# Moving the combining of the first experts' results into the experts' own block of a graph and mixture-of-experts kernel

## The chip, the cores and the metric

The kernel runs on one core of one Trainium2 chip. The metric is the device time of one execution in microseconds (us), from start to end on that core. Lower is better. TensorE is called PE, VectorE DVE, ScalarE ACT, GpSimd POOL and SyncE SP; SPq, ACTq and POOLq are their instruction queues, from which they also issue transfers.

## What is computed

The input x is 3125 rows of 256 numbers. Four layers follow one another, each added to its input, which is normalised (LayerNorm without a gain) beforehand: a graph network of three steps, a first mixture of experts (16 experts, 512 wide, the best two taken for each row), a second graph network with relations, and a second mixture (8 experts, 1024 wide). The change is about the end of the first mixture and the start of the second graph layer:

```python
def _L0_ffn_ref(x, gate_w, gate_b, w1, b1, w2, b2, gamma, beta):
    ...
    topk_w = jax.nn.softmax(topk_vals, axis=-1)
    h = jax.nn.relu(jnp.einsum('bsh,ehf->bsef', x, w1) + b1)
    expert_out = jnp.einsum('bsef,efh->bseh', h, w2) + b2
    sel = jnp.take_along_axis(expert_out, topk_idx[:, :, :, None], axis=2)
    moe = jnp.sum(topk_w[..., None] * sel, axis=2)
    y = x + moe
    mu = jnp.mean(y, axis=-1, keepdims=True)
    var = jnp.var(y, axis=-1, keepdims=True)
    return (y - mu) / jnp.sqrt(var + EPS) * gamma + beta
...
x = x + _L0_ffn_ref(_layernorm(x, axis=-1)[None], ...)[0]
x = x + _L1_gnn_ref(_layernorm(x, axis=-1), edge_index, edge_type_500, ...)
```

The second graph layer gathers a row of h = LayerNorm(x), scaled by a factor of the source node's degree, for each of 103,125 edges, multiplies it by a relation's row and sums by destination. It also needs h itself, for the part of the update that does not pass through the edges.

## The kernel before

Rows are held as NT = 25 tiles of 128 rows, in NJ = 5 groups of J = 5 tiles. `c.x` (in the profile `parts_and_x`) is the running sum, `c.xn` (`xn`) the normalised rows that the experts took in, `c.h` (`h`) the normalised rows for the second graph layer.

**Experts (`experts`, `feed_forward`, L1893).** The rows are sorted by expert into 64 tiles. POOL gathers tile t+4 (L2301) while PE computes tile t: a transpose (L2025), the first product (L2037), the second (L2056); ACT applies the activation (L2122); DVE adds the expert's bias and leaves the result in one of four buffers `f_yb` (L2243); POOL scatters the buffer to DRAM `ys` (L2290), each row to the place of its token, once for the token's first choice and once for its second. POOL at last waits until the scatters have landed, and the block ends. A block ends with all five engines meeting. Then, where a `Core` closes, POOL clears the semaphores that it owned, one after the other, while the others wait (L125), and all meet again.

**Combining (`combine_and_norm`, L2362), a block of its own.** SP reads `ys` back into `got`, ten transfers (five groups, two choices, L2393), then waits for a memset of POOL (L2385), reads the two short tails (L2397), then gamma (L2398) and beta (L2399), both spread over 128 partitions. DVE clips the degrees, ACT takes their root (L2438), and DVE inverts them. DVE waits for gamma and beta, adds beta to all of x (L2514), and goes through the groups in this order, which is written out by hand:

```python
for i in range(NJ):
    sum_up(i)
    if i:
        join(i - 1)
    scale_first(i)
    if i:
        scale_next(i - 1)
join(NJ - 1)
scale_next(NJ - 1)
```

`sum_up` forms y = xn + w0*got0 + w1*got1 (L2472) and its moments (L2456 to L2464); `scale_first` inverts the root that ACT took of the variance (L2412, L2481, L2482); ACT normalises y in place (L2422). `join` multiplies by gamma (L2487), adds to x (L2488) and takes the moments of the new x; `scale_next` makes the next scales (L2497 to L2504). ACT then writes five tiles of rows for the table that the second layer gathers from (L2431, `out`) and, behind them, five tiles of `c.h` (L2435). SP stores each group's `out` (L2403) and waits for the stores; the block and its `Core` end.

**Second graph layer (`aggregate`, L618, and `Beside`, L2565).** 416 steps n of two gathers each (POOL, L705). ACT makes the places of step n (L665, L668) up to six steps ahead of PE, DVE multiplies by the relation's row (L775), PE sums by destination (L794), DVE adds up (L757). Beside these, every 14 steps from step 48 on, one tile of `c.h` goes through a product: PE transposes it (L2612) at step n, ACT copies the transpose (L2633) at step n+4, PE multiplies at n+5 (L2618), DVE adds it to x at n+9 (L2645).

The second experts (L1893 again, with `out` given) end otherwise than the first: there SP itself waits for the scatters (L2284) and then issues the copies of the result (L2016).

Of the kernel before, what the change touches and what calls it, by code (L numbers as in the profile page):

```python
# [7 lines left out]
ALU = mybir.AluOpType  # L8
# [1873 lines left out]
def experts(nc, c, I, name, ne, nf, tiles, softmax_first, w1, b1, w2, b2, logits, xn_table, norm, act_fn, combine_rows, relation=None, out=None):  # L1882

    ys = c.dram(f"{name}_ys", [NP + P if out is not None else 2 * NP + tiles * P, D])
    with Core(nc) as k:
        weight = k.sb(f"{name}_weight", [P, 2, NT])
        slot = k.sb(f"{name}_slot", [P, 2, NT], I32)
        feed_forward(nc, c, name, ne, nf, tiles, softmax_first, logits, w1, b1, w2, b2, norm, act_fn, relation, weight, slot, xn_table, ys, out)
        if combine_rows:
            combine_rows(ys, weight, c.xn)  # L1890


def feed_forward(nc, c, name, ne, nf, tiles, softmax_first, logits, w1, b1, w2, b2, norm, act_fn, relation, weight, slot, xn_table, ys, out):  # L1893
# [9 lines left out]
    with Core(nc) as k:  # L1903
# [17 lines left out]
        low_hit = k.sb(f"{name}_low_hit", [P, 2, NT, P], BF16)  # L1921
        tile_hit = k.sb(f"{name}_tile_hit", [P, 2, NT, tiles], BF16)
        named = k.sb(f"{name}_named", [P, 2, NT, 2, tiles], BF16)
        token_f, token = k.sb(f"{name}_token_f", [P, tiles]), k.sb(f"{name}_token", [P, tiles], I32)
        work = RelationRows(nc, c, k, f"{name}_rr", *relation, True) if relation else None
# [27 lines left out]
        if norm:  # L1953
# [9 lines left out]
            k.sem(f"{name}_e{x}") for x in ("xt", "xT", "h", "hT", "y", "yb", "asked", "ask"))  # L1963
        with nc.Block() as block:  # L1964
# [12 lines left out]
            def _(sp):  # L1977
# [114 lines left out]
            def _(act):  # L2092
# [6 lines left out]
                if not softmax_first:  # L2099
                    act.wait_ge(s_a, 1)  # L2100
                    nc.scalar.activation(small[:, 1, :], small[:, 0, :], ACT.Exp).then_inc(s_b, 1)
                act.wait_ge(s_etab, 1)
                act.wait_ge(s_bias, 16 * len(loads))
                with act.Fori(0, tiles // 2) as i:
                    for s in range(2):
# [12 lines left out]
                        for f in range(FC):  # L2118
                            if f % BF == 0:
# [3 lines left out]
                                                 bias=b1s[:, bass.ds(e, 1), f]).then_inc(s_hT, 1)  # L2123

            @block.vector
            def _(dve):
# [99 lines left out]
                else:  # L2226
# [5 lines left out]
                    v.tensor_tensor(weight[:, 1, :], weight[:, 0, :], small[:, 1, :], ALU.mult)  # L2232
                dve.wait_ge(s_bias, 16 * len(loads))
                dve.wait_ge(s_etab, 1)
                if out is None:
                    dve.sem_inc(s_yb, 2)
                    for t in range(tiles):
                        e = dve.value_load(e_tab[0:1, 0, t:t + 1], min_val=0, max_val=ne - 1)
                        dve.wait_ge(s_y, t + 3)
                        if t >= Y:  # L2240
# [3 lines left out]
                            .then_inc(s_yb, 1)  # L2244
                else:
# [26 lines left out]
            def _(pool):  # L2272
                asked = 0
                if work:
                    while asked < BEFORE:
                        work.both(pool, asked)
                        asked += 1
# [15 lines left out]
                if out is not None:  # L2293
                    pool.wait_ge(s_home, 1)
                    pool.wait_ge(s_start, 32)
                for t in range(tiles):
# [12 lines left out]
                    if work and t >= Q - 1:  # L2309
                        upto = BEFORE + (work.pairs - BEFORE) * (t - Q + 2) // (tiles - Q + 1)  # L2310
                        while asked < upto:
                            work.both(pool, asked)
                            asked += 1
# [8 lines left out]
                if work:  # L2322
                    work.store(pool, work.pairs - 2, work.pairs)
                    work.stored(pool)
# [37 lines left out]
def combine_and_norm(nc, c, name, I, ys, weight, xn, h_table):  # L2362
# [3 lines left out]
    with Core(nc) as k:  # L2366
        k.got = k.sb(f"{name}_got", [P, 2, NT, D])
        k.s_got = [k.sem(f"{name}_got{i}") for i in range(NJ)]
# [389 lines left out]
```

## Time and profile before

| | |
|---|---|
| median of three runs | 3142.7 us (3141.61, 3142.7, 3150.35) |
| the profiled execution, its own time | 3142.47 us |
| its span in the trace | 3140.8 us |
| busy, share of the span | PE 78%, DVE 57%, POOL 56%, ACT 46% |
| mean granted TensorE clock | 0.91 of full speed |
| first experts, 64 tiles | about 1063 to 1377 us |
| combining | 1379.5 us to the stage below |
| second graph layer, first instruction | 1490.17 us |

Times in the trace count from the span's start. The span leaves out 1.7 us of the execution's own time. The execution that was profiled lies 0.2 us under the median.

### The profile page before, as it was taken

The page shows a single profiled execution, that of the slowest core. Times are in us where ns is not written, and L with a number is a line of the kernel's source. Part 1 is how long each engine was busy: PE and PEld are TensorE (multiplying, and loading weights), DVE is VectorE, ACT ScalarE, POOL GpSimd, SP SyncE. Part 2 cuts the span into 40 slices and gives each one's busy share as a digit, 9 for nine tenths or more (in the row PEclk, how much of TensorE's full clock was granted, in tenths as well). Part 3 has the DMA queues.
Part 4 walks back from the last instruction along what each step waited for, and adds up shares of the span by engine and source line. Part 5 has one row for each costly group of instructions (what it writes and reads, how often), then busy time and mean ns, then how long its engine had stood idle before and what let it go on. Part 6 is the DMA issues. An engine that isn't in the chain of part 4 may idle for free. (4 is left out here: it accounts for less than half of the span.)

```text
span 3140.8 us, 53019 instructions
## 1 busy us (share of the span) xinstructions
PE 2446.1 (78%) x14195; PEld 1912.7 (61%) x14195; DVE 1785.5 (57%) x5112; ACT 1454.7 (46%) x3766; POOL 1747.2 (56%) x1701
## 2 busy tenths in 40 slices
PE   1549999989998489840587787778777767699997
PEld 1226666667777488740465565555555545699996
DVE  5649989847788511018676666666666666401110
ACT  0247767645665333315544444444434434355553
POOL 1547777667774045420777777777777760133332
PEclk9979999999999599975899999998999897799998
DMA  5657777568885233431766666666666642243232
GB/s 204 232 161 218 231 222 213 171 215 258 262 251 170 81 120 108 160 115 44 221 189 186 186 189 178 186 184 186 184 180 184 181 135 99 90 130 75 51 63 65
DMA packets 289373, 516.56 MB, mean 164 GB/s; under 512 B 79344, under 2 KB 137057, under 8 KB 287084
## 3 DMA queue, kind: packets, MB, share of 16 engines
q0 software_dynamic: 86192, 225.20, 28.0%
q1 hardware_dynamic: 184380, 265.72, 25.8%
q10 hardware_dynamic: 18544, 22.59, 2.2%
q8 instruction: 116, 1.90, 0.2%
q14 instruction: 141, 1.16, 0.1%
HBM read 381.08 MB, written 137.11 MB: 165 GB/s over the span
## 5 line engine op out<-in xcount | busy, mean ns | idle before, releaser
L705 POOL DMA_INDIRECT agg_r_rows<-h_table,parts_and_x x832 | 832.2, 1000 | 364.9 <-issue 227.4
L794 PE MATMUL agg_r_sums<-agg_r_rows,agg_r_onehot 128*128 128x257 f32 x1664 | 497.8, 428 | 255.7 <-DVE agg_r_rows L775 162.9
L794 PEld LDWEIGHTS agg_r_sums<-agg_r_rows,agg_r_onehot 128*128 128x128 f32 x1664 | 312.6, 207 | 395.0 <-issue 315.8
L665 ACT ACTIVATE agg_r_gap<-iota,parts_and_x 128x128 f32<-128x128 f32 x832 | 286.8, 392 | 450.2 <-PE agg_r_sums L794 421.2
L757 DVE TENSOR_TENSOR acc<-acc,agg_r_sums 128x257 f32 (+1 forms) x834 | 351.5, 421 | 134.5 <-PE agg_r_sums L794 47.4
L1651 POOL DMA_INDIRECT rl_buf<-r_table,kinds x288 | 315.4, 1095 | 140.4 <-issue 72.0
L2037 PEld LDWEIGHTS f_pH<-f_xT,f_w 128*128 128x128 f32 x2816 | 329.7, 193 | 36.4 <-ACT f_xT L2116 15.6
L2037 PE MATMUL f_pH<-f_xT,f_w 128*128 128x128 f32 x2816 | 343.5, 279 | 7.5 <-ACT f_xT L2113 4.6
L808 PE MATMUL agg_r_spread<-xn 128*128 128x257 bf16 x2664 | 344.5, 289 | 0.0
L2056 PE MATMUL f_pY<-f_w,f_hT 128*128 128x256 f32 x1408 | 324.3, 380 | 9.0 <-DMA f_w<-in_L_ffn_w 9.0
L808 PEld LDWEIGHTS agg_r_spread<-xn 128*128 128x128 bf16 x2664 | 276.4, 104 | 72.2 <-issue 8.8
L2122 ACT ACTIVATE f_hT<-f_pH,f_b 128x128 f32<-128x128 f32 x704 | 198.1, 373 | 260.9 <-PE f_pH L2037 260.6
L1456 PE MATMUL la_acc<-la_parts,la_counts 128*128 128x512 f32 x1250 | 309.1, 404 | 12.0 <-DVE la_parts L1563 12.0
L1651 POOL DMA_INDIRECT rm_buf<-r_table,kinds x250 | 245.9, 984 | 88.2 <-issue 69.2
L2056 PEld LDWEIGHTS f_pY<-f_w,f_hT 128*128 128x128 f32 x1408 | 258.3, 190 | 41.1 <-DMA f_w<-in_L_ffn_w 10.8
L1456 PEld LDWEIGHTS la_acc<-la_parts,la_counts 128*128 128x128 f32 x1250 | 235.0, 190 | 72.7 <-issue 25.0
L2301 POOL DMA_INDIRECT f_xb<-xn_table,f_token x120 | 118.5, 988 | 267.7 <-DVE f_token L2206 116.5
L1370 DVE TENSOR_SCALAR b_oh<-b_numbers,b_code 128x400 bf16<-128x400 f16 x980 | 253.5, 323 | 0.0
L775 DVE TENSOR_TENSOR agg_r_rows<-agg_r_rows,agg_r_rel 128x514 f32<-128x514 f32 x305 | 210.9, 691 | 55.9 <-DMA agg_r_rows<-h_table,parts_and_x 54.7
L1249 PE MATMUL b_strips<-b_oh,b_at 128*128 128x400 bf16 x980 | 200.1, 335 | 53.1 <-DVE b_oh L1370 46.3
L2284 POOL DMA_INDIRECT f_ys<-f_yb,f_home x56 | 88.2, 1576 | 270.9 <-DVE f_yb L2269 262.4
L2263 DVE TENSOR_TENSOR f_plain<-f_pY,f_b 128x256 f32<-128x256 f32 x56 | 23.8, 424 | 359.4 <-PE f_pY L2056 359.4
(418 smaller groups left out, 3678.4 us busy)
## 6 DMA issues: line engine op xcount, KB each, us to landing
agg_r_rel<-relation_rows SPq DMA_DIRECT2D x305, 260.0 KB, 3.0
relation_rows<-rl_buf SPq DMA_DIRECT2D x144, 260.0 KB
relation_rows<-rm_buf SPq DMA_DIRECT2D x125, 260.0 KB, 3.3
agg_r_rows<-h_table,parts_and_x POOLq DMA_INDIRECT x832, 3.4
f_w<-in_L_ffn_W SPq DMA_DIRECT2D x18, 512.0 KB, 5.3
f_w<-in_L_ffn_W SPq DMA_DIRECT2D x9, 1024.0 KB, 4.9
f_w<-in_L_ffn_w SPq DMA_DIRECT2D x30, 256.0 KB, 3.0
f_w<-in_L_ffn_w SPq DMA_DIRECT2D x15, 512.0 KB, 3.7
```

The source lines that it names most:

```text
L665: last = nc.scalar.activation(gap[:, n % HOT, t, :], c.iota[:, 0:P], ACT.Abs, bias=c.tab["b_near"][:, column(g) + t:column(g) + t + 1])
L705: pool.indirect_dma_start(rows[:, n % SLOTS, t, :], None, table, bass.IndirectOffsetOnAxis(ap=indices[:, t:t + 1], axis=0)).then_inc(s_row ...
L757: v.tensor_tensor(here, here, sums[:, (2 * (n - LAG) + t) % BANKS, 0:used], ALU.add).then_inc(s_acc, 1)
L775: last = v.tensor_tensor(here, here, rel[:, n % SLOTS, :, 0:used], ALU.mult)
L794: last = nc.tensor.matmul(sums[:, (2 * n + t) % BANKS, 0:used], onehot[:, n % HOT, t, :], rows[:, n % SLOTS, t, 0:used], start=True, stop= ...
L808: last = nc.tensor.matmul(spread[:, t, 0:used], hot[:, r % 2, q, t * P:(t + 1) * P], parts[:, q, part, 0:used], start=q == 0 and part == 0 ...
L1249: last = nc.tensor.matmul(strips[:, n % BANKS, 0:CODES], at[:, n % 2, t, :], oh[:, n % 2, t, :], start=t == 0, stop=t == DEEP - 1)
L1370: last = v.tensor_scalar(oh[:, n % 2, t, :], numbers[:, :], code[:, q, 1, own, t:t + 1], None, ALU.is_equal)
L1456: last = nc.tensor.matmul(acc[:, n % 2, :], counts[:, i, j, :], parts[:, s, :], start=s == 0, stop=s == NT - 1)
L1651: pool.indirect_dma_start(self.buf[:, n, g, :], None, self.table, bass.IndirectOffsetOnAxis(ap=self.c.kinds[:, at:at + 1], axis=0)).then_i ...
L2037: last = nc.tensor.matmul(pH[s][:, f * P:(f + 1) * P], w1b[:, s, f // (FC // 2), at:at + P], xT[:, s, h, :], start=h == 0, stop=h == KD - 1)
L2056: last = nc.tensor.matmul(pY[s][:, 0:D], hT[:, s, f, :], w2b[:, s, f, :], start=f == 0, stop=f == FC - 1)
```

## The change

The combining moves into the experts' block. A class `Finish` holds what it needs; its parts are called from the five engines' programs of `feed_forward`. The room for `got` is the memory of two tables that the sorting is done with, and `c.h`; the room for `out` is that of the experts' biases. Arithmetic stays the same. In detail:

```diff
@@ feed_forward
-        low_hit = k.sb(f"{name}_low_hit", [P, 2, NT, P], BF16)
+        hits_room = k.sb(f"{name}_hits", [P, NT * (P + 2 * tiles)])
...
+            got = [hits_room[:, 0:NT * D].rearrange("p (t d) -> p t d", d=D), c.h[:, :, :]]
+            finish = Finish(nc, c, k, name, I, ys, weight, got, b2s[:, :, :].rearrange("p e d -> p (e d)"), h_table)
@@ SP
                     sp.dma_start(to, what, allow_slow_non_contiguous=True).then_inc(s_bias, 16)
+                if finish:
+                    finish.ask(sp)
...
                     second(tiles - 2 + s, s)
+                if finish:
+                    for s in range(Y):
+                        sp.wait_ge(s_added[s], 16 * (tiles // Y))
+                    finish.sync(sp)
@@ ACT
+                if finish:
+                    finish.degrees(act)
                 act.wait_ge(s_etab, 1)
...
+                if finish:
+                    finish.scalar(act)
@@ DVE
+                if finish:
+                    finish.inverse(dve, v, st)
                 dve.wait_ge(s_bias, 16 * len(loads))
...
                             .then_inc(s_yb, 1)
+                        finish.shift(dve, v, t)
+                    dve.wait_ge(s_yb, tiles + 2)
+                    finish.vector(dve, v, st)
@@ POOL
+                else:
+                    finish.clear_rest(pool)
                 for t in range(tiles):
...
-                if out is None:
-                    for s in range(Y):
-                        pool.wait_ge(s_added[s], 16 * (tiles // Y))
@@ new: Finish
+    def ask(self, sp):
+        sp.dma_start(self.gamma[:, :], row(self.I["L0_ffn_gamma"])).then_inc(self.s_gb, 16)
+        sp.dma_start(self.beta[:, :], row(self.I["L0_ffn_beta"])).then_inc(self.s_gb, 16)
+    def clear_rest(self, pool):
+        for rows in self.got:
+            pool.memset(rows[:, NT - 1, :], 0.0).then_inc(self.s_rest, 1)
+    def degrees(self, act):
+        act.wait_ge(self.s_clip, 1)
+        self.nc.scalar.activation(self.clip[:, :, :], self.clip[:, :, :], ACT.Sqrt).then_inc(self.s_degrees, 1)
+    def inverse(self, dve, v, st):
+        v.tensor_scalar_max(self.clip[:, :, :], self.c.deg[:, :, 0:NT], 1.0).then_inc(self.s_clip, 1)
+        dve.wait_ge(self.s_degrees, 1)
+        v.reciprocal(self.c.norm_dst[:, :], self.clip[:, 1, :])
+        st.link(v.reciprocal(self.c.norm_src[:, :], self.clip[:, 0, :]))
+        dve.wait_ge(self.s_gb, 32)
+    def shift(self, dve, v, t):
+        if t < NT:
+            v.tensor_tensor(self.c.x[:, t, :], self.c.x[:, t, :], self.beta[:, :], ALU.add).then_inc(self.s_shift, 1)
+    def sync(self, sp):
+        sp.wait_ge(self.s_rest, 2)
...
+    def scalar(self, act):
+        def normalise(i):
+            act.wait_ge(self.s_var1, i + 1)
+            nc.scalar.activation(self.root[:, 0, :], self.var[:, 0, :], ACT.Sqrt).then_inc(self.s_root1, 1)
+            act.wait_ge(self.s_down1, i + 1)
...
+        def next_rows(i):
+            act.wait_ge(self.s_var2, i + 1)
+            nc.scalar.activation(self.root[:, 1, :], self.var[:, 1, :], ACT.Sqrt).then_inc(self.s_root2, 1)
+            act.wait_ge(self.s_down2, i + 1)
...
+        for i in range(NJ):
+            normalise(i)
+            if i:
+                next_rows(i - 1)
+        next_rows(NJ - 1)
+    def vector(self, dve, v, st):
...
+        for i in range(NJ):
+            sum_up(i)
+            if i:
+                if i >= 2:
+                    scale_next(i - 2)
+                join(i - 1)
+            scale_first(i)
+            if i:
+                moments(c.x, 1, i - 1).then_inc(self.s_var2, 1)
+        scale_next(NJ - 2)
+        join(NJ - 1)
+        moments(c.x, 1, NJ - 1).then_inc(self.s_var2, 1)
+        scale_next(NJ - 1)
@@ Beside.tensor
         if (t := self.tile(n, 0)) is not None:
+            pe.wait_ge(self.s_even, t + 1)
             pe.wait_ge(self.s_turned, t + 2)
@@ Beside.scalar
+        if (t := self.tile(n, -6)) is not None:
+            nc.scalar.activation(self.c.h[:, t, :], self.c.x[:, t, :], ACT.Identity, bias=self.c.h_down[:, t:t + 1],
+                                 scale=self.c.h_rstd[:, t:t + 1]).then_inc(self.s_even, 1)
```

`sync` issues the same ten transfers, the two tails behind them, and the five stores. `next_rows` makes `out` alone: the 25 activations that write `c.h` are now among ACT's steps of the second layer, six steps ahead of the transpose that reads them. `c.h_rstd` and `c.h_down` keep their scales. The relation work that `feed_forward` could do beside the experts was passed to neither of its two calls, and its code goes.

## Rows read from the trace of the kernel before

**Rows 1.** Windows: stretch, length, busy PE, PEld, DVE, ACT, POOL, granted clock, DMA share, GB/s

```profile
1376.00:1490.00 114.00, 0.00 (x0) 0.00 (x0) 72.95 (x224) 41.03 (x87) 0.53 (x1) 0.50 0.27 88
...
1900.00:2200.00 300.00, 235.83 (x1278) 175.35 (x1276) 203.11 (x522) 127.70 (x354) 229.71 (x231) 0.91 0.66 184
...
1385.00:1390.00 5.00, 0.00 (x0) 0.00 (x0) 0.00 (x0) 0.00 (x0) 0.00 (x0) 0.50 1.10 349
```

**Rows 2.** Timeline, 1372 to 1413: start us, us, engine, line, operation, [idle before, releaser]

```profile
1372.43 0.97 POOL L2290 DMA_INDIRECT f_ys<-f_yb,f_home  x1 [1.11 <-DVE f_yb L2243]
1379.47 13.23 SPq L2393 DMA_DIRECT2D f_got<-f_ys  x10
1405.44 7.10 DVE L2514 TENSOR_TENSOR parts_and_x<-parts_and_x,f_beta 128x1280 f32<-128x1280 f32 x5 [23.90 <-DMA f_beta<-in_L_ffn_beta]
1412.57 2.07 DVE L2472 SCALAR_TENSOR_TENSOR f_got<-f_got,f_weight,xn 128x256 f32<-128x256 f32 x5
```

**Rows 3.** The block's boundary, line L125, SP's queue and POOL's, 1370 to 1382

```profile
L125 SPq DRAIN  x1: 7/7/7, 1377.2 to 1377.2; - x1
...
L125 POOLq DRAIN  x1: 34/34/34, 1379.2 to 1379.2; - x1
```

**Rows 4.** Timeline at the end of the second experts

```profile
3122.06 1.54 POOL L2284 DMA_INDIRECT f_ys<-f_yb,f_home  x1 [2.97 <-DMA f_ys<-f_yb,f_home]
3125.82 3.14 SPq L2016 DMA_DIRECT2D out<-f_ys  x5
```

**Rows 5.** The first three of the ten loads (L2393): durations ns, starts, landing

```profile
L2393 SPq DMA_DIRECT2D f_got<-f_ys x3: 401/518/519, 1379.5 to 1380.5; - x3
...
DMA to landing us min/median/max: 4.5/6.0/7.3
```

**Rows 6.** Timeline of one turn of DVE's loop in the combining, 1420 to 1433.4

```profile
1420.00 2.06 DVE L2472 SCALAR_TENSOR_TENSOR f_got<-f_got,f_weight,xn 128x256 f32<-128x256 f32 x5
...
1426.75 1.48 DVE L2487 TENSOR_TENSOR f_got<-f_got,f_gamma 128x1280 f32<-128x1280 f32 x1
...
1429.79 1.73 DVE L2456 BATCH_NORM_STATS2 f_stats<-parts_and_x 128x6 f32<-128x256 f32 x5
...
1432.70 0.19 DVE L2497 RECIPROCAL f_rstd<-f_root 128x5 f32<-128x5 f32 x1
...
1433.35 2.06 DVE L2472 SCALAR_TENSOR_TENSOR f_got<-f_got,f_weight,xn 128x256 f32<-128x256 f32 x5
```

**Rows 7.** Timeline of the combining's end and the second layer's first instruction

```profile
1475.41 1.49 DVE L2487 TENSOR_TENSOR f_got<-f_got,f_gamma 128x1280 f32<-128x1280 f32 x1 [1.92 <-ACT f_got L2422]
...
1478.46 1.73 DVE L2456 BATCH_NORM_STATS2 f_stats<-parts_and_x 128x6 f32<-128x256 f32 x5
...
1482.07 2.56 ACT L2431 ACTIVATE f_out<-parts_and_x,f_down_src,f_rstd_src 128x256 f32<-128x256 f32 x5 [0.73 <-DVE f_down_src L2500]
...
1490.17 0.36 SPq L680 DMA_DIRECT2D xn<-r_table  x1
```

**Rows 8.** The last of the five stores of rows (L2403), SP's queue

```profile
1484.70 0.36 SPq L2403 DMA_DIRECT2D h_table<-f_out  x1
```

**Rows 9.** POOL's memset of the combining (L2385)

```profile
L2385 POOL MEMSET f_got<- x1: 525/525/525, 1379.5 to 1379.5; 128x512 f32 x1
```

**Rows 10.** Timeline of the experts' start: DVE's last small step and ACT's first copy

```profile
1104.42 0.18 DVE L2232 TENSOR_TENSOR f_weight<-f_weight,f_small 128x25 f32<-128x25 f32 x1
...
1107.81 0.45 ACT L2116 ACTIVATE f_xT<-f_pX 128x128 f32<-128x128 f32 x2 [4.09 <-PE f_pX L2025]
```

**Rows 11.** Timeline of one tile of the experts, DVE and POOL

```profile
1125.51 0.42 DVE L2243 TENSOR_TENSOR f_yb<-f_pY,f_b 128x256 f32<-128x256 f32 x1 [3.31 <-PE f_pY L2056]
1126.75 0.98 POOL L2290 DMA_INDIRECT f_ys<-f_yb,f_home  x1 [1.45 <-DVE f_yb L2243]
```

**Rows 12.** The 25 activations that write h, in the combining

```profile
L2435 ACT ACTIVATE h<-parts_and_x,f_down,f_rstd x25: 583/584/587, 1437.7 to 1486.5; 128x256 f32<-128x256 f32 x25
```

**Rows 13.** Waits between 1550 and 2600: who waited for whom, sum, times, longest

```profile
ACT be_hT L2633 <- PE be_turns L2612: 134.6, 25, 9.5
```

More of the change, by code:

```diff
@@ L1879, in _, with experts @@
                         nc.scalar.activation(shift[:, :], vecs[:, 4, :], ACT.Sqrt).then_inc(s_root, 1)
-def experts(nc, c, I, name, ne, nf, tiles, softmax_first, w1, b1, w2, b2, logits, xn_table, norm, act_fn, combine_rows, relation=None, out=None):
+def experts(nc, c, I, name, ne, nf, tiles, softmax_first, w1, b1, w2, b2, logits, xn_table, norm, act_fn, h_table=None, out=None):
     ys = c.dram(f"{name}_ys", [NP + P if out is not None else 2 * NP + tiles * P, D])
@@ L1887, in experts, with feed_forward @@
         slot = k.sb(f"{name}_slot", [P, 2, NT], I32)
[L1888 to L1893, printed above, removed]
+        feed_forward(nc, c, I, name, ne, nf, tiles, softmax_first, logits, w1, b1, w2, b2, norm, act_fn, weight, slot, xn_table, ys, h_table, out)
+def feed_forward(nc, c, I, name, ne, nf, tiles, softmax_first, logits, w1, b1, w2, b2, norm, act_fn, weight, slot, xn_table, ys, h_table, out):
     FC, Q, Y = nf // P, 4, 4
@@ L1920, in feed_forward @@
         split = k.sb(f"{name}_split", [P, 2, 2, NT], BF16)
-        low_hit = k.sb(f"{name}_low_hit", [P, 2, NT, P], BF16)
+        hits_room = k.sb(f"{name}_hits", [P, NT * (P + 2 * tiles)])
+        hits_b = hits_room[:, :].bitcast(BF16)
+        low_hit = hits_b[:, 0:2 * NT * P].rearrange("p (q t l) -> p q t l", q=2, t=NT)
+        named = hits_b[:, 2 * NT * P:2 * NT * (P + 2 * tiles)].rearrange("p (q t a b) -> p q t a b", q=2, t=NT, a=2)
         tile_hit = k.sb(f"{name}_tile_hit", [P, 2, NT, tiles], BF16)
-        named = k.sb(f"{name}_named", [P, 2, NT, 2, tiles], BF16)
         token_f, token = k.sb(f"{name}_token_f", [P, tiles]), k.sb(f"{name}_token", [P, tiles], I32)
-        work = RelationRows(nc, c, k, f"{name}_rr", *relation, True) if relation else None
         w1b = k.sb(f"{name}_w1", [P, 2, 2, KD * nf // 2])
@@ L1963, in feed_forward @@
             k.sem(f"{name}_e{x}") for x in ("xt", "xT", "h", "hT", "y", "yb", "asked", "ask"))
+        finish = None
+        if out is None:
+            got = [hits_room[:, 0:NT * D].rearrange("p (t d) -> p t d", d=D), c.h[:, :, :]]
+            finish = Finish(nc, c, k, name, I, ys, weight, got, b2s[:, :, :].rearrange("p e d -> p (e d)"), h_table)
         with nc.Block() as block:
@@ L2272, in _ @@
             def _(pool):
[L2273 to L2277, printed above, removed]
                 def add_rows(t):
@@ L2308, in _ @@
                         put_rows(t - Q)
[L2309 to L2313, printed above, removed]
                 for t in range(tiles - Q, tiles):
@@ L2707, in build @@
         c.h = c.sb("h1", [P, NT, D])
+        c.h_rstd, c.h_down = c.sb("h1_rstd", [P, NT]), c.sb("h1_down", [P, NT])
         h1_table = c.dram("h1_table", [NP, W1])
-        def finish0(ys, weight, xn):
-            combine_and_norm(nc, c, "f0", I, ys, weight, xn, h1_table)
         experts(nc, c, I, "f0", E0, F0, TILES0, False, I["L0_ffn_w1"], I["L0_ffn_b1"], I["L0_ffn_w2"], I["L0_ffn_b2"],
-                logits[0], xn_table, None, ACT.Relu, finish0)
+                logits[0], xn_table, None, ACT.Relu, h1_table)
         gnn1(nc, c, I, r_table, relation_rows, h1_table, logits[1], xn_table)
         experts(nc, c, I, "f1", E1, F1, TILES1, True, I["L1_ffn_W1"], I["L1_ffn_b1"], I["L1_ffn_W2"], I["L1_ffn_b2"],
-                logits[1], xn_table, (I["L1_ffn_ln_g"], I["L1_ffn_ln_b"]), ACT.Gelu, None, None, out)
+                logits[1], xn_table, (I["L1_ffn_ln_g"], I["L1_ffn_ln_b"]), ACT.Gelu, None, out)
 def kernel(**inputs):
```

232 lines of the change are left out of this document (88 added, 144 removed).

## The prediction

> **What bounds the kernel now.** I began with the busy time by stretch. From 1376 to 1490 us, 114 us, TensorE does nothing, POOL almost nothing, and DVE is busy for 73 us [rows 1]: the combining covers no other work, so every microsecond taken out of its path should come out of the total. Next I read the timeline for what that path is. Its first part is waiting. The last scatter of expert results is issued at 1372.43, the loads of these results begin at 1379.47, and DVE's first large instruction, the addition of beta, starts only at 1405.44, released by beta's load; the first sum starts at 1412.57 [rows 2]. SP's queue issues ten loads, two tails and gamma ahead of beta, and all are served at 349 GB/s [rows 1], so that the smallest transfer comes last. From 1412.57 on DVE goes through its groups without a gap, one each 13.35 us (1420.00 to 1433.35) [rows 6]; ACT's activations fit beneath. At the end one DVE wait of 1.92 us shows [rows 7]. The last store is issued at 1484.70 [rows 8] and the second graph layer starts at 1490.17 [rows 7].
>
> **How early the loads start.** Now SP itself waits for the scatters. The end of the second experts shows this hand-over: SP issues 3.76 us after the start of POOL's last scatter, 2.22 us after its end [rows 4]. From POOL's end here (1372.43 + 0.97 = 1373.40 [rows 2]) 2.22 gives 1375.6. By the start it would be 1376.2; the latest is 1377.2, when SP has passed the first meeting of the boundary [rows 3]; the earliest is 1373.40 itself. I take 1375.6, because the two scatters differ in length. One cost comes before: POOL's two memsets of 256 columns now stand between the token list and the first gather, with PE waiting. One of 512 columns takes 0.525 us [rows 9]; two halves cost at least that and at most 1.05. I take 0.6, and all later work slips by it. Issue: 1376.2.
>
> **How early the first sum starts.** It needs two loads. The second is issued 0.40 us after the first and lands 6.0 us later [rows 5]: 6.4. Ends: 4.5, as if the first alone counted, and 1.0 + 7.3 = 8.3, as the third load landed. First sum at 1382.6, where it was at 1412.57: **30.0 us gained**. By parts: 3.85 of boundary (1375.6 to 1379.47), 19.55 of DVE's wait for beta beyond the first pair (1405.44 - 1379.47 - 6.4), 7.13 of beta's addition (1412.57 - 1405.44), less 0.6. The later pairs are never late: two loads of 0.655 MB at 349 GB/s take 3.8 us, and DVE takes a pair each 13.35.
>
> **What goes beside the experts.** Adding beta becomes 25 DVE instructions of 128x256. The bias addition of that shape takes 0.42 us and is followed by a wait for PE; in the row it had waited 3.31 us [rows 11]. Cover: that wait; without it, 25 x 0.42 = 10.5 us. The clip, the root and the inverses come when DVE has finished the weights at 1104.60, and ACT's first copy is at 1107.81 [rows 10]; a root, and even its table load, lie in between. Cost nothing; without that cover at most as long again, 3.2 us (1107.81 - 1104.60). Gamma and beta are asked for at the start of the block, while SP waits for the expert table. Taking `got` into the memory of the sorting tables costs no new wait: these were read before the first gather.
>
> **DVE's loop in the new order.** The same instructions: sums 6.75 (1420.00 to 1426.75), join 3.04 (to 1429.79), moments of x and first scale 2.91 (to 1432.70), next scale 0.65 (to 1433.35), 13.35 together [rows 6]. The first turn takes 7.43 (1412.57 to 1420.00). Four turns follow, of which only three now hold a next scale: 4 x 13.35 - 0.65 = 52.75. So 60.2 us after the first sum's start the loop is done. Is ACT in time? It gets the next scale, writes five rows (2.56 [rows 7]) and takes a root, some 2.8; DVE's join beside it takes 3.04. Margin 0.25; if I am wrong, up to 0.5 in each of three turns, 1.5. The tail: ACT's normalising of the last group (2.56) now runs beside DVE's moments, where DVE waited 1.92 for it. I allow 0.3 for the root behind it, then 0.65 next scale, 3.05 join (1475.41 to 1478.46), 3.61 moments, root and scale (to 1482.07), 2.63 until the store is issued (to 1484.70) [rows 7, 8]: 10.24. In all 70.4 where it was 1484.70 - 1412.57 = 72.1: **1.7 gained**. Last store: 1453.0.
>
> **The end.** From the last store to the second layer 5.47 us passed. One thing is added: the experts' semaphores are now cleared here. At the old boundary this is POOL's stretch from 1377.2 to 1379.2 [rows 3]: **2.0 lost**. Combining's own semaphores are as many as before, within one. Second layer: 1453.0 + 5.5 + 2.0 = 1460.5, against 1490.17. The removed h activations give nothing of their own: the last ended at 1487.1 [rows 12], while the boundary was waiting for the store.
>
> **h in the second layer.** 25 activations of 0.584 us [rows 12]. ACT is busy for 128 of 300 us there [rows 1] and stands 134.6 us in 25 waits for PE's transpose [rows 13], four steps after it. The new activation comes ten ACT steps before that wait, while ACT runs up to six steps ahead of PE, so neither PE's new wait nor the places behind the activation should be late. Cost nothing; without cover 25 x 0.584 = 14.6 us.
>
> **The sum.** 30.0 + 1.7 - 2.0 = 29.7 us. The profiled execution took 3142.47 us (span 3140.8); less 29.7 it is 3112.8. The median of the runs is 0.2 above it, which I leave out: **3112.8 us**.
>
> **Rivals.**
>
> *Beta's additions hold up POOL* (5%). POOL moves the rows in and out in the experts, and an addition may fall on it. POOL has 1.45 us of idle per tile before its scatter [rows 11], against 0.42: against. If all 25 are paid: 3123.3. The Trainium skill, "SBUF — State Buffer", section "Who interferes with whom", would have such an addition, both inputs in SBUF, block a POOL instruction that reads SBUF for its whole length. By that rule at most 10.5 us is at stake, the same number; no row here shows whether a scatter's issue counts as such a reader.
>
> *h is paid for in the second layer* (5%). ACT's work falls in front of places that PE needs. For: PE is held by other engines there, 235.8 busy of 300 [rows 1]. Against: ACT's lead. 3112.8 + 14.6 = 3127.4.
>
> *The first sum waits for the whole queue* (3%). If the loads interleave and the first pair comes with the last, the first sum starts as late after the issue as beta landed, 26.0 instead of 6.4: 19.6 lost, 3132.4. Against: landings of 4.5, 6.0 and 7.3 in order [rows 5].
>
> *Slower: the wait for h closes a ring* (2%). Place: PE's new wait before the transpose, and ACT's old wait for that transpose, in order with the places of the steps between. If ACT reached h(t) only when PE stood there, PE would lose part of the stand that ACT has now, 134.6 / 25 = 5.4 us per tile; in full 3112.8 + 134.6 = 3247. It decides against the change above 29.7 / 25 = 1.2 us per tile. Against: ten steps between the two.
>
> *The change does not do what it says* (3%). If a wait that I do not see keeps the combining behind a full boundary and beta late, no change: 3142. The idle PE from 1376 to 1490 speaks against anything else having hidden the stage.
>
> **How the numbers follow.** 82% for my sum. Its own range: start of the loads -2.2/+1.6, first pair -1.9/+1.9, memsets +0.4, ACT +1.5, clears and boundary +/-1, and a second layer of 1100 us that may shift by 2 or 3; not all at once: 3107 to 3119. To hold 8 in 10 with the smaller shortfalls I give 3107 to 3121. About 0.3%, 9.4 us, is what a measurement of this kernel can tell from no change. Faster by more, below 3133.3: my case and the first three rivals, 0.95. Same 0.03, slower 0.02.
>
> **What would show each step.** The loads issued about 1376 with no L125 row between them and the last scatter. The first sum 6.4 us later, no wait for beta. 25 additions of 0.42 in the experts, each behind a bias addition, the tiles as far apart as before. A DVE turn of 13.35 without waits for ACT above 0.3. The last store near 1453, the second layer near 1460.5 with 7.5 between. 25 activations for h after step 42, no row in which PE waits for them. I am wrong if the stage begins near 1460 and the end does not follow (second layer), or if the first sum comes late (loads), or if turns lengthen (ACT's order).

## The result and the profile after

| | before | after |
|---|---|---|
| median | 3143.95 us (3141.61 to 3150.35, four runs) | 3113.26 us (3111.5 to 3116.89, four runs) |
| the profiled execution, its own time | 3142.47 us | 3116.89 us |
| its span in the trace | 3140.8 us | 3115.3 us |
| ratio of the times, 95% interval | | 0.9903 (0.989 to 0.9915) |

The medians are 30.7 us apart; 29.7 was forecast, and the time, 3112.8, was 0.5 us off. That closeness is partly luck: the four runs after lie 5.4 us apart, and two terms of the sum missed in the same direction. The two profiled executions are only 25.5 us apart, because the one profiled after was the slowest of its four. So the stage itself has to be read in the trace, and what the rest of the kernel does beside it has to be kept apart from that.

The page of the kernel after, part 1. TensorE was 78% busy before: nothing was taken from it, the span is shorter.

```profile
span 3115.3 us, 53042 instructions
...
PE 2448.7 (79%) x14195; PEld 1913.7 (61%) x14195; DVE 1785.7 (57%) x5132; ACT 1454.2 (47%) x3766; POOL 1754.5 (56%) x1702
```

Windows of after, columns as in [rows 1]. In 78 us of combining DVE is now busy for 64.6, where before it was busy for 73.0 of 114: it is the bound from the first sum on.

```profile
1376.00:1454.00 78.00, 0.00 (x0) 0.00 (x0) 64.63 (x215) 27.32 (x60) 0.00 (x0) 0.50 0.36 117
```

Timeline of after, from the last scatter to the first sum; it answers to [rows 2].

```profile
1374.20 0.97 POOL L2303 DMA_INDIRECT f_ys<-f_yb,f_home  x1 [0.75 <-DVE f_yb L2258]
1376.77 0.40 SPq L2418 DMA_DIRECT2D f_hits<-f_ys  x1
...
1383.20 2.07 DVE L2479 SCALAR_TENSOR_TENSOR f_hits<-f_hits,f_weight,xn 128x256 f32<-128x256 f32 x5 [9.63 <-DMA h<-f_ys]
```

No boundary stands between the first two rows: 2.57 us from the start of the scatter to the first load, where it was 7.04. The third row waits for a load of results, not for beta: 6.43 us after the issue, where it was 33.10.

One turn of DVE's loop and the chain's end, timelines of after, as [rows 6] and [rows 7, 8].

```profile
1403.28 2.06 DVE L2479 SCALAR_TENSOR_TENSOR f_hits<-f_hits,f_weight,xn 128x256 f32<-128x256 f32 x5
...
1410.69 1.48 DVE L2486 TENSOR_TENSOR f_hits<-f_hits,f_gamma 128x1280 f32<-128x1280 f32 x1
1410.73 2.56 ACT L2450 ACTIVATE f_b<-parts_and_x,f_down_src,f_rstd_src 128x256 f32<-128x256 f32 x5 [7.12 <-DVE f_down_src L2506]
...
1413.20 0.19 ACT L2435 ACTIVATE f_root<-f_var 128x5 f32<-128x5 f32 x1
...
1413.73 0.19 DVE L2494 RECIPROCAL f_rstd<-f_root 128x5 f32<-128x5 f32 x1
...
1443.54 0.19 DVE L2503 RECIPROCAL h_rstd<-f_root 128x5 f32<-128x5 f32 x1 [0.27 <-ACT f_root L2443]
...
1453.48 0.36 SPq L2425 DMA_DIRECT2D h_table<-f_b  x1
1460.94 0.37 SPq L680 DMA_DIRECT2D xn<-r_table  x1
```

The next turn begins at 1416.58, so a turn is 13.30. ACT's root at 1413.20 comes 0.5 before DVE inverts it at 1413.73, with no wait in brackets. In the tail 0.27 of waiting is left of 1.92.

The boundary of after, line L125. Before, SP's queue and POOL's were 2.0 us apart at the boundary between the blocks [rows 3] and 1.4 at the one behind the combining; now there is one boundary, and they are 3.4 apart.

```profile
L125 SPq DRAIN  x1: 7/7/7, 1457.3 to 1457.3; - x1
...
L125 POOLq DRAIN  x1: 41/41/41, 1460.7 to 1460.7; - x1
```

Beside the experts: the memsets, a tile and the roots (timelines of after, as [rows 10, 11]).

```profile
1101.84 0.31 POOL L2394 MEMSET f_hits<- 128x256 f32 x1 [115.64 <-DVE f_token L2219]
1102.09 0.41 POOL L2394 MEMSET h<- 128x256 f32 x1
1102.65 0.96 POOL L2316 DMA_INDIRECT f_xb<-xn_table,f_token  x1 [0.16 <-issue]
...
1104.73 0.32 DVE L2403 RECIPROCAL norm_dst<-f_clip 128x25 f32<-128x25 f32 x1 [0.46 <-ACT f_clip L2398]
...
1107.73 0.45 ACT L2127 ACTIVATE f_xT<-f_pX 128x128 f32<-128x128 f32 x2 [3.02 <-PE f_pX L2034]
...
1123.56 0.42 DVE L2258 TENSOR_TENSOR f_yb<-f_pY,f_b 128x256 f32<-128x256 f32 x1 [3.24 <-PE f_pY L2065]
1123.91 0.41 DVE L2409 TENSOR_TENSOR parts_and_x<-parts_and_x,f_beta 128x256 f32<-128x256 f32 x1
1124.81 1.00 POOL L2303 DMA_INDIRECT f_ys<-f_yb,f_home  x1 [1.70 <-DVE f_yb L2258]
```

In the second layer, h (L2634, first row, of the line's own view) and ACT's wait for the transpose (second row, of the waits from 1461 to 2566), which answers to [rows 13].

```profile
L2634 ACT ACTIVATE h<-parts_and_x,h_down,h_rstd x25: 583/585/587, 1569.2 to 2444.6; 128x256 f32<-128x256 f32 x25
```

```profile
ACT be_hT L2640 <- PE be_turns L2616: 122.9, 25, 7.8
```

**Where the 25.5 us of this pair come from.** From the last scatter's start to the second layer's first instruction 117.7 us became 86.7: 31.0 gained. From the first gather to the last scatter 269.3 became 271.6, and, the gather being 0.4 earlier, the last scatter is 1.8 later. The second graph layer took 1103.8 instead of 1101.0, 2.8 lost, and what follows it 0.9. 31.0 - 1.8 - 2.8 - 0.9 = 25.5.

### The profile page after: what moved, and what is told of

Read it like the earlier page. It is cut to its first block and busy times, and to the rows that moved or that the text cites. A ratio compares the mean times of both kernels' runs of the same rounds, so it can differ in the third digit from the quotient of the medians.

```text
span 3115.3 us, 53042 instructions
## 1 busy us (share of the span) xinstructions
PE 2448.7 (79%) x14195; PEld 1913.7 (61%) x14195; DVE 1785.7 (57%) x5132; ACT 1454.2 (47%) x3766; POOL 1754.5 (56%) x1702
## 3 DMA queue, kind: packets, MB, share of 16 engines
q8 instruction: 117, 1.92, 0.2%
## 5 line engine op out<-in xcount | busy, mean ns | idle before, releaser
L1496 ACT ACTIVATE la_counts<-matrix 128x640 fp32r<-128x640 fp8e4 x250 | 183.9, 737 | 94.8 <-PE la_acc L1456 85.1
```

## The experiments

All are compared with runs of the kernel before on the same chip: "ratio" is the time divided by that kernel's, with its 95% interval. The kernel before took 3148.81 us (median) beside the first four, 3143.3 beside the next four and 3148.43 beside the last two. Times expected from 3113 therefore come out some 5 us higher in the first four and the last two, and there the ratio is what counts. "Stage" is the time from the start of the last scatter to the first instruction of the second graph layer: 117.7 in before, 86.7 in after. My theory was the prediction's: the wait for beta, its addition and the boundary were the gain, and everything that was moved out lies under other work. The rivals: fewer blocks are the gain, whatever the order of the loads; the new order of DVE and ACT carries it; h or beta is paid for elsewhere.

### Beta late again, in the new block

```diff
@@ feed_forward, SP
-                if finish:
-                    finish.ask(sp)
@@ Finish.sync, behind the two tails
+        self.ask(sp)
@@ DVE: no shift(t) beside the experts; in vector(), ahead of the loop
+        dve.wait_ge(self.s_gb, 32)
+        for i in range(NJ):
+            ts = self.tiles_of(i)
+            last = v.tensor_tensor(c.x[:, ts, :], c.x[:, ts, :], bc(self.beta[:, :].unsqueeze(1), [P, J, D]), ALU.add)
```

> The changed kernel, with gamma and beta asked behind the twelve loads again and beta added in five instructions when it has landed, as before the change. The boundary stays away. My theory (wait for beta 19.6 us beyond the first pair, its addition 7.1 us): first sum 26 us after the first load's issue plus 7.1, so some 26 us later than in the changed kernel, and the whole about 3113 + 26 = 3139 us. Rival (the gain came from the boundary that went, the queue's order mattered little): within 5 us of the changed kernel, 3113 to 3118.

Ratio 0.9984 (0.9971 to 0.9997), 3144.08 us. Timeline, from the first load to the first sum:

```profile
1375.61 0.40 SPq L2414 DMA_DIRECT2D f_hits<-f_ys  x1
...
1395.46 0.43 SPq L2387 DMA_DIRECT2D f_beta<-in_L_ffn_beta  x1
1401.59 7.10 DVE L2513 TENSOR_TENSOR parts_and_x<-parts_and_x,f_beta 128x1280 f32<-128x1280 f32 x5 [29.18 <-DMA f_beta<-in_L_ffn_beta]
1408.72 2.07 DVE L2476 SCALAR_TENSOR_TENSOR f_hits<-f_hits,f_weight,xn 128x256 f32<-128x256 f32 x5
```

The loads start as early as in after and the first sum comes 33.1 us behind them, the very figure of before. The stage is 113.4, 26.7 longer than after's. Without the early beta only 4.3 of the 31.0 are left; 4.5 of boundary and 1.9 of order, less 2.0 of clears, make 4.4. Fewer blocks alone is not the gain. The rows also show what beta waits for: of the 26.0 us from the first load to its landing, 19.85 pass before SP issues it (1375.61 to 1395.46), and only 6.1 from its issue to its landing. So the wait is spent ahead of the issue, while SP issues the larger transfers. Whether SP is itself held back by the transfers under way, and whether beta asked for from another engine's queue would have come early too, was not tried.

### The kernel before, with gamma and beta asked for first

```diff
@@ combine_and_norm, SP
             def _(sp):
+                sp.dma_start(g[:, :], row(I["L0_ffn_gamma"])).then_inc(s_gb, 16)
+                sp.dma_start(b[:, :], row(I["L0_ffn_beta"])).then_inc(s_gb, 16)
                 for i in range(NJ):
...
-                sp.dma_start(g[:, :], row(I["L0_ffn_gamma"])).then_inc(s_gb, 16)
-                sp.dma_start(b[:, :], row(I["L0_ffn_beta"])).then_inc(s_gb, 16)
```

> The kernel before, with one edit: SP asks for gamma and beta ahead of the ten loads. My theory: beta lands some 6 us after the block begins and its addition (7.1 us) runs while the loads land, so the first sum starts 6 + 7 = 13 to 14 us after the block's start where it was 33: 19 us gained, about 3124 us. Rival (the boundary is what mattered): no more than 5 us gained, 3138 or above.

Ratio 0.9936 (0.9916 to 0.9957), 3128.26 us. Timeline:

```profile
1373.40 0.97 POOL L2290 DMA_INDIRECT f_ys<-f_yb,f_home  x1 [1.11 <-DVE f_yb L2243]
1380.44 0.35 SPq L2389 DMA_DIRECT2D f_gamma<-in_L_ffn_gamma  x1
...
1381.32 13.72 SPq L2395 DMA_DIRECT2D f_got<-f_ys  x9
1384.99 7.10 DVE L2514 TENSOR_TENSOR parts_and_x<-parts_and_x,f_beta 128x1280 f32<-128x1280 f32 x5 [2.47 <-DMA f_beta<-in_L_ffn_beta]
1392.12 2.07 DVE L2472 SCALAR_TENSOR_TENSOR f_got<-f_got,f_weight,xn 128x256 f32<-128x256 f32 x5
```

Two lines that change place give a stage of 96.4: 21.4 of the 31.0 us. I had expected 19; the medians, 3128.26 and 3148.81, are 20.5 apart. What is left of the change is 4.4 of boundary (7.04 still stands between the first two rows), 5.3 of beta's addition and its wait (11.7 from the block's start to the first sum, against 6.4), 1.9 of order, less 2.0 of clears: 9.6, and 31.0 - 21.4 = 9.6.

### h written in the block again

```diff
@@ Finish.scalar, at the end of next_rows(i)
+            for t in range(i * J, i * J + J):
+                nc.scalar.activation(c.h[:, t, :], c.x[:, t, :], ACT.Identity, bias=c.h_down[:, t:t + 1], scale=c.h_rstd[:, t:t + 1])
@@ Beside
-            pe.wait_ge(self.s_even, t + 1)
...
-        if (t := self.tile(n, -6)) is not None:
-            nc.scalar.activation(self.c.h[:, t, :], ...
```

> The changed kernel with the 25 activations for h back in the combining, each group's behind its rows, and none in the second layer, PE's wait for them gone. The changed kernel's second layer took 2.8 us longer from its first instruction to the first transpose of the next stage (1103.8 against 1101.0). My theory: h costs the second layer nothing, so this length stays within what executions differ by, and the combining grows because five h activations (2.6 us) and five rows (2.6) and a root exceed DVE's join of 3.0: DVE waits about 2.3 us in each of three turns, 7 us in all; total about 3120. Rival (h is paid for in the second layer): its length falls by 2.8 or more, up to 14.6, and the total is at most 3117.

Ratio 0.9931 (0.9913 to 0.9948), 3124.88 us. The first sum to the last store is 76.9 us, 6.6 more than in after. The waits of the stage name who is late, a wait that after has only once, with 0.3 us:

```profile
DVE f_rstd L2496 <- ACT f_root L2435: 7.0, 4, 2.2
```

ACT writes two sets of rows a turn (2 x 2.56) ahead of the root that DVE asks for. So the new order of DVE leaves no room for h on ACT, and moving h out is part of what makes it good. The second layer without h was not shorter: 1105.4.

### h twice in the second layer

The same activation once more, into spare memory that nothing reads, ahead of the real one.

```diff
@@ Beside.scalar
         if (t := self.tile(n, -6)) is not None:
+            nc.scalar.activation(self.spare[:, :], self.c.x[:, t, :], ACT.Identity, bias=self.c.h_down[:, t:t + 1],
+                                 scale=self.c.h_rstd[:, t:t + 1])
```

> The changed kernel with the activation for h made twice in each of its 25 places of the second layer, once into spare memory. My theory (hidden under ACT's lead): within 2 us of the changed kernel, 3111 to 3115. Rival (on the path): another 3 us if the 2.8 us of the profile are h's cost, 14.6 us if all of it is paid: 3116 to 3128.

Ratio 0.9909 (0.9888 to 0.9931), 3119.29 us, with a stage as in after (86.8). The time lies above the 3111 to 3115 that I expected and inside the rival's range, but the unchanged kernel took 3119.08 on the same chip (the last experiment), so it does not speak for the rival. The second layer took 1105.0, and 1105.4 with no h in it. Its length moves by more than this from one execution to the next: the layer without h took 1101.0, 1101.3 and 1105.4; with h once 1095.5 to 1107.8 in eight traces. The means are 1102.6 without and 1102.7 with h once. No price of h is to be seen above that, and 14.6 us would be; a price of 2 or 3 us is not excluded by these lengths.

### More additions beside the experts

Behind the tiles from 2 on DVE adds two more rows of 128x256, both inputs in SBUF, into spare memory: 124 instructions beside the 25.

```diff
@@ Finish.shift
+        if t >= 2:
+            dve.wait_ge(self.s_more, 2 * (t - 2))
+            for s in range(2):
+                v.tensor_tensor(self.spare[:, s, :], self.c.xn[:, t % NT, :], self.beta[:, :], ALU.add).then_inc(self.s_more, 1)
```

> The changed kernel with two more additions of 128x256, both inputs in SBUF, behind the bias addition of each of the experts' tiles 2 to 63 (their results go to spare memory). My theory (hidden under DVE's wait for PE): from the first gather to the last scatter of the experts 271 to 273 us as in the five traces so far, total 3111 to 3119. Rival (DVE's additions hold up POOL's transfers of rows): 124 additions of 0.42 us, up to 52 us longer; at a tenth of it 5 us.

Ratio 0.9897 (0.9881 to 0.9914), 3111.44 us. First gather to last scatter is 271.8 us; this length moves by itself, 269.3 in before and 271.6 in the second experiment, whose experts are before's, 271.6 and 269.6 in the changed kernel's two traces. Timeline of one tile:

```profile
1221.82 0.42 DVE L2258 TENSOR_TENSOR f_yb<-f_pY,f_b 128x256 f32<-128x256 f32 x1 [2.90 <-PE f_pY L2065]
1222.16 0.75 DVE L2414 TENSOR_TENSOR f_spare<-xn,f_beta 128x256 f32<-128x256 f32 x2
1223.06 0.98 POOL L2303 DMA_INDIRECT f_ys<-f_yb,f_home  x1 [1.72 <-DVE f_yb L2258]
```

DVE's wait for PE shrinks by about what is added. In this tile the additions fall between the end of the bias addition (1222.24) and the start of the scatter (1223.06), a stretch in which POOL does not yet transfer, and the scatter takes the same 0.98 us. In the changed kernel all 25 additions of beta fall so: none of them overlaps a gather or a scatter. In tiles 2 to 24 of this run, with three additions each, the last one reaches 0.18 us into the scatter:

```profile
1145.33 0.75 DVE L2414 TENSOR_TENSOR f_spare<-xn,f_beta 128x256 f32<-128x256 f32 x2
1145.90 1.04 POOL L2303 DMA_INDIRECT f_ys<-f_yb,f_home  x1 [1.66 <-DVE f_yb L2258]
```

These 23 scatters take 1.04 to 1.05 us, the same ones in after 0.99, and POOL's idle time hides that. The second layer, where DVE multiplies rows of 128x514 with both inputs in SBUF, shows what such a meeting costs (timeline of before):

```profile
1631.71 0.68 DVE L775 TENSOR_TENSOR agg_r_rows<-agg_r_rows,agg_r_rel 128x514 f32<-128x514 f32 x1
1631.80 1.42 POOL L705 DMA_INDIRECT agg_r_rows<-h_table,parts_and_x  x1 [0.30 <-issue]
```

A transfer that POOL begins while DVE's instruction runs ends 0.83 us behind DVE's end here, and 0.81 to 0.84 in all 91 such cases in after that had 0.3 us or more of DVE's instruction still to come (from 1560 to 2500; 1.12 to 1.49 us each instead of 0.95). One that begins before DVE's instruction mostly keeps its length. So the rival's mechanism is there; beta's additions do not meet it, because they end before the scatter begins. Paid in full they would cost 10.5 us.

### The old order of DVE and ACT in the new block

```diff
@@ Finish.vector
             if i:
-                if i >= 2:
-                    scale_next(i - 2)
                 join(i - 1)
+                moments(c.x, 1, i - 1).then_inc(self.s_var2, 1)
             scale_first(i)
             if i:
-                moments(c.x, 1, i - 1).then_inc(self.s_var2, 1)
-        scale_next(NJ - 2)
+                scale_next(i - 1)
@@ Finish.scalar: the second root of group i - 1 ahead of normalising group i
```

> The changed kernel with DVE's and ACT's order in the combining as before the change (join with the moments behind it, then the first scale, then the next scale of the same group; ACT takes both roots ahead of its rows). h stays in the second layer. My theory: from the first sum to the last store 72.1 us in place of 70.3, 1.8 us longer, in the trace; the total is 3113 to 3117, too close to tell by itself. Rival (the new order is needed once h is gone, or saves much more): more than 75 us.

Ratio 0.9916 (0.9899 to 0.9932), 3113.11 us. The first sum to the last store is 72.2 us (1376.79 to 1448.95), as in before (72.1); after has 70.3. The order is worth 1.9 us, no more, and only together with the other half of the change: the old order takes 72.1 with h in the block and 72.2 without, the new order 76.9 with h and 70.3 without. By totals this can't be told from after (its interval covers 0.9903); only the trace tells it.

### Gamma on POOL

This and the next two were to beat the change. POOL is idle in the stage, so it multiplies by gamma.

```diff
@@ Finish: new, called at the end of POOL's program
+    def times(self, pool):
+        for i in range(NJ):
+            rows = self.got[0][:, self.tiles_of(i), :]
+            pool.wait_ge(self.s_even, (i + 1) * J)
+            pool.tensor_tensor(rows, rows, bc(self.gamma[:, :].unsqueeze(1), [P, J, D]), ALU.mult).then_inc(self.s_times, 1)
@@ join
-            dve.wait_ge(self.s_even, (i + 1) * J)
-            st.link(v.tensor_tensor(y[:, ts, :], y[:, ts, :], bc(self.gamma[:, :].unsqueeze(1), [P, J, D]), ALU.mult))
+            dve.wait_ge(self.s_times, i + 1)
```

> The changed kernel with the multiplication by gamma (five of 128x1280, 1.48 us each on DVE) done by POOL in place. POOL is idle in the combining. My theory: DVE's turn falls from 13.3 to 11.8 us if POOL's instruction is done before DVE's sums of the next group are, 6 us gained over the stage less the last group's longer wait, so 4 us, total about 3109. Rival (POOL's reading holds up DVE's instructions with two SBUF inputs, or POOL takes longer than a turn): no gain, or the stage is longer than in the changed kernel.

A miss: ratio 0.9953 (0.9937 to 0.997), 3127.71 us, the first sum to the last store 79.3, 9.0 longer instead of 4 shorter. Timeline of the first turn, then the sums' line by itself (duration in ns: shortest, median, longest):

```profile
1386.85 4.69 DVE L2488 SCALAR_TENSOR_TENSOR f_hits<-h,f_weight,f_hits 128x256 f32<-128x256 f32 x5
1387.52 2.94 POOL L2418 TENSOR_TENSOR f_hits<-f_hits,f_gamma 128x1280 f32<-128x1280 f32 x1 [18.19 <-ACT f_hits L2448]
```

```profile
L2488 DVE SCALAR_TENSOR_TENSOR f_hits<-f_hits,f_weight,xn x25: 470/477/3104, 1377.3 to 1434.0; 128x256 f32<-128x256 f32 x25
L2488 DVE SCALAR_TENSOR_TENSOR f_hits<-h,f_weight,f_hits x25: 471/479/3102, 1379.4 to 1436.1; 128x256 f32<-128x256 f32 x25
```

A sum that falls beside POOL's multiplication (2.9 to 3.0 us) takes 3.10 instead of 0.48: DVE stands until POOL is done. In the last turn a product of 128x5 that reads nothing of POOL's ends 0.03 us after it:

```profile
1445.71 2.88 POOL L2418 TENSOR_TENSOR f_hits<-f_hits,f_gamma 128x1280 f32<-128x1280 f32 x1 [12.67 <-ACT f_hits L2448]
...
1446.08 2.54 DVE L2512 TENSOR_TENSOR h_down<-f_mean,h_rstd 128x5 f32<-128x5 f32 x1
```

The Trainium skill, "SBUF — State Buffer", section "Who interferes with whom", has it so: a DVE instruction with two inputs in SBUF and a GpSimd one that reads there exclude each other for their whole length. The trace agrees: here DVE waits for POOL. In sum: the 50 sums take 31.2 us instead of 20.7, the five small products of 128x5 are 2.4 longer, all of it in the one just shown (2.54 instead of 0.17), and DVE stands 3.9 more ahead of its inverses, 16.8 together, for the 7.4 of gamma (5 x 1.48) that left DVE; 9.4 worked out, 9.0 measured.

### Gamma on POOL, a split first pair, early clears

On top of the last: the first two loads are cut into tiles 0 to 1 and 2 to 4, and POOL clears 26 semaphores of the experts while DVE works on the groups.

```diff
@@ Finish.sync
+        for a, b, sem in ((0, 2, self.s_early), (2, J, self.s_got[0])):
+            for q in range(2):
+                sp.dma_start(self.got[q][:, a:b, :], ys[q * NP + a * P:q * NP + b * P, :].rearrange("(t p) d -> p t d", p=P)).then_inc(sem, 16)
@@ POOL, ahead of finish.times(pool)
+                    pool.wait_ge(finish.s_root1, 1)
+                    for sem in gone:
+                        pool.sem_clear(sem)
+                        k.sems.remove(sem)
```

> As gamma on POOL, and two more edits: the first pair of loads is split (tiles 0 and 1 first, DVE sums them while tiles 2 to 4 land), and POOL clears 26 of the experts' semaphores while the combining runs, not behind it. Expected on top of the run with gamma on POOL: 1.5 to 2 us earlier first sum, 1.9 us less between the last store and the second layer (5.6 in place of 7.5); total about 3105.

A miss as well: ratio 0.9938 (0.9916 to 0.9959), 3123.91 us where 3105 was expected, because the multiplication on POOL was still in it. Timeline, the split:

```profile
1378.10 0.40 SPq L2433 DMA_DIRECT2D f_hits<-f_ys  x1
...
1381.63 0.88 DVE L2503 SCALAR_TENSOR_TENSOR f_hits<-f_hits,f_weight,xn 128x256 f32<-128x256 f32 x2 [6.73 <-DMA h<-f_ys]
...
1386.05 1.28 DVE L2503 SCALAR_TENSOR_TENSOR f_hits<-f_hits,f_weight,xn 128x256 f32<-128x256 f32 x3 [2.62 <-DMA h<-f_ys]
```

The first sum starts 3.5 us after the issue instead of 6.4, but then DVE stands 2.62 for tiles 2 to 4, and the first group's root comes 13.25 after the issue, where it came 13.31: the split gives nothing. The early clears do: from the last store to the second layer 5.6 us instead of 7.6 in the run before this one.

### Early clears alone

```diff
@@ POOL, at the end of feed_forward's program
+                if finish:
+                    pool.wait_ge(finish.s_root1, 1)
+                    for sem in gone:      # 26 semaphores of the experts
+                        pool.sem_clear(sem)
+                        k.sems.remove(sem)
```

> The changed kernel with one edit: POOL, idle in the combining, clears 26 of the experts' semaphores once ACT has taken the first root there, in place of behind the combining. Mine: from the last store to the second layer 5.6 us in place of 7.5, everything else as in the changed kernel, total 2 us lower than the changed kernel beside it. Rival (the clears were hidden behind the store's landing): no change of the 7.5.

Ratio 0.9894 (0.9879 to 0.9909), 3112.87 us. Timeline, the last store and the second layer:

```profile
1453.81 0.36 SPq L2433 DMA_DIRECT2D h_table<-f_b  x1
1459.29 0.37 SPq L680 DMA_DIRECT2D xn<-r_table  x1
```

5.48 us, as in before (5.47), against 7.46: the 2.0 that the change paid for its clears is won back.

### The change again, beside the last

The kernel after, unchanged.

> The changed kernel once more, unedited, as the neighbour of the run with early clears and as a second trace of it. From the first gather of the experts to the last scatter 269 to 273 us, by when TensorE's clock rises; first sum to last store 70.3; second layer to the next stage's first transpose 1101 to 1105.5; total 3113, within 0.2%.

Ratio 0.9906 (0.9892 to 0.992), 3119.08 us; the first sum to the last store 70.3, then 7.5 to the second layer, as in the first trace of it. The second layer took 1106.8, a little more than the 1101 to 1105.5 expected. The intervals of this and of the early clears overlap, so the 2 us are shown in the trace and not by totals. The early clears have the lowest ratio of the set, beat the kernel before beyond doubt, and beat the change in the trace alone.

## Why the prediction was right

| step | predicted us | measured us |
|---|---|---|
| scatter's start to first load, gained | 3.9 | 4.5 |
| first load to first sum | 6.4 | 6.43 |
| the same, gained | 26.7 | 26.7 |
| POOL's memsets, lost | 0.6 | 0.1 |
| first sum to last store, and gained | 70.4, 1.7 | 70.3, 1.9 |
| one turn of DVE | 13.35 | 13.30 |
| last store to second layer, and lost | 7.5, 2.0 | 7.46, 2.0 |
| beta beside the experts, 25 instructions | 0 | none to be seen |
| h in the second layer, 25 activations | 0 | none to be seen |
| sum, gained | 29.7 | 31.0 in the stage, 30.9 with the memsets |

*Start of the loads.* I priced it from POOL's end, 2.22 us, by the end of the second experts [rows 4]. It was 1.60 (1374.20 + 0.97 = 1375.17 to 1376.77), and 2.5 to 2.6 from the scatter's start in every trace with the new block. 2.22 was 0.6 too much, inside the range that I gave it.

*The memsets*, which stand ahead of the stage, are the one term that was wrong in kind. I charged their whole length, 0.6. POOL had needed 0.81 us from the list's end to its first gather before; with the two memsets in between it needed 0.87. They fill a gap that was there. These two terms make up the shortfall, 0.6 and 0.5 us of the 1.2 between 29.7 and 30.9.

*The first sum* at 6.4 came from counting two landings at their places in the queue [rows 5], and the order of landings held. The rival of the interleaved queue (19.6 lost) is out by this row alone.

*The order* was summed from the instructions of one turn and one tail, and the sum was 0.1 off. The allowance for ACT's lateness was not needed: the turns show no ACT wait above 0.3. The third experiment shows how thin that cover is, since h put back on ACT makes DVE wait four times, 7.0 in all.

*Beta* and *h* were costed at nothing with their covers named. The sum named DVE's wait for PE as beta's cover; just as much it is POOL's pause between the bias addition and the scatter, which stood only under the rival: all 25 additions end in it. A DVE instruction of this kind that is running when POOL begins a transfer does hold it up, as the fifth experiment's rows show, so it is the timing that makes beta free. 124 more additions leave the experts as long as they were. h is written some 30 us before PE reads it (the first at 1569.2, its transpose at 1600.0); h once, twice and not at all gives a second layer within what it varies by. For PE no row shows a wait for h, and the ring of the slower rival did not close: ACT's wait for the transpose fell from 134.6 to 122.9, about by what the new activations take (25 x 0.585 = 14.6).

*The clears* were priced from the old boundary, and the price held. The ninth experiment takes 26 of them away from the boundary, and 1.98 of the 2.0 comes back.

*Most of the gain was the order of two small loads.* The second experiment reaches 21.4 of 31.0 us with two lines moved. The prediction had this (19.55 of waiting as the largest term), and it is worth saying apart, since the merging of the blocks, the bulk of the code, brings the smaller part.

What stays open: the experts are 2.2 us longer and the second layer 2.8 in the profiled pair. Both lie within what executions differ by: over the twelve traces the experts took 269.3 to 273.3 and the second layer 1095.5 to 1107.8, and the changed kernel's own second profile has 269.6 and 1106.8. What moves them I have not shown.

## What to carry to other kernels

One engine issues its transfers one after the other: look at which transfer the first consumer needs, and issue the smallest of them first; that was two thirds of this gain. Price a merged stage by its chain (hand-over, first landing, turns, tail, boundary), with each term from a row of the same kernel, and write down the cover of every edit that costs nothing; what was cleared or set up at an old boundary still has to be done, and can be given to an engine that is idle before the new one. An idle POOL is not free help for a busy DVE: while it multiplied rows in SBUF, a DVE instruction with two inputs there stood still.

## What the runs showed of the hardware

**POOL and DVE hold each other up**. DVE stands while POOL multiplies in SBUF, as told above: 3.10 us in place of 0.48. The other way round, POOL's issuing of an indirect transfer is held up by a DVE instruction with two inputs in SBUF that is already running: it ends 0.81 to 0.84 us behind DVE's end, up to 1.49 us instead of 0.95. Whoever begins first goes first; a transfer that had begun before DVE's instruction mostly kept its 0.95 to 1.00 us (156 of 169 in after), and DVE's instruction its 0.68 to 0.70.

**The clock's rise falls on either side of one product.** At the experts' start, after TensorE had stood for 5.9 us in before and 6.3 in after, the second tile's first product (16 matmuls) took 2.05 us in five of the twelve traces and 3.53 to 3.79 in the other seven; the changed kernel's two profiles have one of each. Windows of before and then of after, columns as in [rows 1]; the figure behind POOL's is the granted clock.

```profile
1107.00:1113.00 6.00, 4.54 (x20) 3.90 (x20) 0.00 (x0) 1.35 (x6) 1.76 (x2) 0.61 0.74 235
1113.00:1118.00 5.00, 4.37 (x29) 3.81 (x30) 0.22 (x1) 2.16 (x9) 0.00 (x0) 1.00 0.62 210
```

```profile
1107.00:1113.00 6.00, 4.90 (x20) 4.10 (x20) 0.00 (x0) 1.29 (x6) 1.35 (x2) 0.50 0.62 207
1113.00:1118.00 5.00, 4.31 (x21) 4.26 (x22) 0.00 (x0) 1.04 (x6) 0.00 (x0) 0.57 0.61 210
```

From 1113 to 1118 the clock is 1.00 in the first, the full 2.4 GHz, and 0.57 in the second, for the most part still 0.50, the lower level of 1.2 GHz. The product costs 1.7 us more so. It is not the change's doing, as the kernel has both; nor does it settle how long the experts are, which with the short product took 269.3 and 269.6 in two traces and 271.8 to 272.3 in three.

**Issuing slows as large transfers follow one another.** A load of results takes SP's queue 0.40 us to issue at first and 1.5 to 1.9 from the fifth on (1376.77 and 1379.45 to 1388.63 in after). Gamma and beta are of one size; behind the loads gamma's issue took 2.46 us (in the first experiment), ahead of them 0.35 (in the second). Why was not tested. The first pair is out before the slowing begins.
